# Flamingo block on one core: context 1 scaled on VectorE, x of batch 0 freed of its magic numbers on TensorE, the router's exponential moved into unit 0

## The chip, the core and the metric

One core of one Trainium2 chip. Its engines are TensorE (PE, with a weight loader, PEld), VectorE (DVE), ScalarE (ACT), GpSimd (POOL) and SyncE (SP), which issues transfers. Each runs its own list of instructions in order and waits on semaphores for the others. The metric is the time of one execution on the device, in microseconds (us).

## The reference

Four batches of 256 tokens with 256 features. The block is two gated residual steps:

```python
x = x + jnp.tanh(g_xattn[0]) * _L0_xattn_ref(_layernorm(x, axis=-1), ctx_2048)
x = x + jnp.tanh(g_ffn[0]) * _L0_ffn_ref(_layernorm(x, axis=-1), ...)
```

The first step multiplies, for each batch, the normalised x with that batch's context (256x256). Both are first rounded to 8-bit floats (4 exponent, 3 mantissa bits) and scaled back: x with one scale per token and 128 features, the context with one per 128x128 block. The second is a mixture of 8 experts of width 176 with the 4 best per token, plus a shared expert of width 704 under a sigmoid gate. The expert weights come from a softmax over router logits, so the router needs exponentials; each expert is silu(x @ wg) * (x @ wu) @ wd.

## The kernel before, in words

Everything is written out by hand: each engine has its own list, and the order in it is the order of the source.

**The attention step.** Tokens lie on the partitions, in 8 tiles of 128; a batch is two tiles. DVE takes mean and variance; ACT writes `xc`, the centred x (`centre`), and scales it to the 8-bit range (`scale_x`); contexts are scaled likewise in `cw` (`scale_ctx`, four instructions of 128 columns, one for each 128x128 block). Rounding to 3 mantissa bits is done with magic numbers: a DVE step masks the exponent bits of the value (`exponents`), a step makes of that power of two a large number (`magic` on ACT with Relu; for context 0 `magic_ctx` on DVE), and two DVE steps add it and subtract it again (`rounded`, or `round_ctx` for context 0), which leaves the rounded value in bf16 (`xq`, `cq`). For batches 0 and 1 PE transposes `xq` into PSUM (`transpose_xq`), ACT copies it to `xqt` (`copy_xqt`), and PE multiplies it with `cq` (`attend`, `attend_by_tiles`). For batches 2 and 3 transfers do the transposing.

The dequantised sum x + attention is built in parts: ACT scales the product's first half of features into `y2` (`residual0`), DVE adds the second to x (`residual1`), and a last add joins them: on POOL for batch 0 (`residual_sum_0`), on DVE for batch 1 (`residual_sum`, L812). Then come the second layer norm (`stats_x1`; `inverse_std1` on POOL, L350; `norm_x1`, L825), transposes on PE, and `h_hi` and `h_lo`, the normalised tokens as a sum of two fp32r numbers (`high_h`, `high_h_by_blocks`, `low_h`).

**Fillers.** Between the head's products PE runs products whose result nobody reads (`keep_clock_up`, L1206): 2 before `attend_by_tiles(1)`, 9 behind it, then 4, 2 and 1.

**The feed-forward step** handles the tokens in two halves of 512, and for each half the 17 slices of 128 hidden rows: 34 units, numbered n. A unit is `gate(n)` (6 products of 512 columns), `up(n)` (6) and `down(n-1)` (6), each product in three passes of high and low parts (L1143 for gate and up, L1248 to L1256 for down). ACT makes the high parts of the weights (`high_gu`, L531; `high_d`, L535), the silu and the high part of the activation (`high_a`, L552). POOL makes the low parts of the weights (`low_gu`, L362; `low_d`, L375; `low_first` for unit 0, in two pieces, L369). DVE multiplies (`gated`, L897) and makes the low part (`low_a`, L906). `gate(n)` waits for POOL's low part of its weights, and that for ACT's high part. Each half's router runs amid its first units: logits (`first_products`), `copy_logits`, transposes, `route_compare` (which ends in `ex_in`, L856, before `gt`), the exponential on ACT (`exp_router`, L515), `route_rank` (L862 to L864), `route_weigh`. Second-half batches 2 and 3 go through the attention step in between units 3 to 16 of the first half.

Silu and Exp are in different tables of ACT. A table load is an instruction of its own in the trace (ACT_TABLE_LOAD). At the start one is asked for by hand (`preload_act_table`, L438), others stand in front of the activation that needs them.

The last stage is `finish(1, ...)`: for each of two blocks of 128 output features, DVE adds the product to the residual (L936) and SP stores it.

## Time and profile before

| | |
|---|---|
| median of 3 runs | 175.09 us (174.53 to 175.18) |
| the profiled execution | 174.99 us |
| its span, first to last instruction | 172.8 us |
| mean granted TensorE clock | 1.000 |
| busy: PE, PEld | 154.2 us, 122.6 us |
| busy: DVE, ACT, POOL | 123.2 us, 103.9 us, 81.1 us |
| read from HBM, written | 21.51 MB, 1.09 MB |

An engine's busy time is the time covered by its instructions. Times of instructions count from the span's start. A row of a timeline merges neighbours of one form (x4), and in brackets gives the idle time before it and what released it. The chain of waits goes back from the last instruction to what released each step. "L1143" is line 1143 of the kernel before.

### The profile page before, as it was taken

To read this page: it belongs to the slowest core of one execution; us is meant where nothing else is said; L and a number is where in the kernel's file an instruction comes from. 1 tells how busy PE (TensorE), PEld (TensorE's weight loads), DVE (VectorE), ACT (ScalarE), POOL (GpSimd) and SP (SyncE) were. 2 spreads that over 40 slices of the span, in tenths; PEclk is the share of its full clock that TensorE was granted. 3 is DMA by queue.
4 is the path that set the end of the run, shared out by engine and by line. 5 is a ranking of instruction groups with operands and counts; after the bars stand their busy time and mean duration, and the time that the engine had idled before them with its cause. 6 is when DMAs were issued, how large, how long until landed. Compare 5 with 4: busy or idle time off the path is not lost.

```text
span 172.8 us, 2338 instructions
## 1 busy us (share of the span) xinstructions
PE 154.2 (89%) x700; PEld 122.6 (71%) x700; DVE 123.2 (71%) x258; ACT 103.9 (60%) x223; POOL 81.1 (47%) x103
## 2 busy tenths in 40 slices
PE   0033979999999999999999999999999999999991
PEld 0022447787888887877788888888888888888880
DVE  1899882897779889988989667943486655444553
ACT  2588843578668699656375545884654444554530
POOL 4350564245673565563346444353665554444410
PEclk9999999999999999999999999999999999999999
DMA  4499920000499994134423325205999100000003
GB/s 129 130 392 402 399 101 0 2 4 4 113 277 236 351 401 176 23 114 133 154 83 119 79 70 206 95 4 106 265 246 334 52 4 0 0 0 2 0 0 121
DMA packets 12768, 23.00 MB, mean 133 GB/s; under 512 B 3266, under 2 KB 4290, under 8 KB 12756
## 3 DMA queue, kind: packets, MB, share of 16 engines
q1 hardware_dynamic: 12180, 22.34, 41.1%
q10 hardware_dynamic: 576, 0.52, 1.1%
q8 instruction: 5, 0.08, 0.2%
q14 instruction: 7, 0.06, 0.1%
HBM read 21.51 MB, written 1.09 MB: 131 GB/s over the span
## 4 chain that ended last, share of the span: by engine, by line
PE 83%; DVE 6%; ACT 2%; POOL 2%; DMA 2%; issue 2%; DVEq 1%; POOLq 0%
PE bank L1143 52%; PE bank L1248 4%; PE bank L1252 4%; PE bank L1250 4%; PE bank L1249 4%; PE bank L1255 4%; PE bank L1256 4%; DMA x<-xs 2%; PE bank L1119 1%; POOL rstd L350 1%; DVE amax_x L777 1%; PE bank L1265 1%; POOL x L356 1%; ACT xc L461 1%; ACT y L486 1%
## 5 line engine op out<-in xcount | busy, mean ns | idle before, releaser
L362 POOL TENSOR_TENSOR w_lo<-w_raw,w_hi 128x512 fp32r<-128x512 f32 (+1 forms) x33 | 41.6, 1260 | 49.9 <-ACT w_hi L531 49.9
L1143 PE MATMUL bank<-h_hi,w_hi 128*128 128x512 f32 x130 | 51.5, 396 | 0.0
L1143 PE MATMUL bank<-h_hi,w_lo 128*128 128x512 f32 x130 | 50.7, 390 | 0.0
L1143 PE MATMUL bank<-h_lo,w_hi 128*128 128x512 f32 x130 | 50.6, 390 | 0.0
L552 ACT ACTIVATE a_hi<-bank 128x512 fp32r<-128x512 f32 (+1 forms) x34 | 20.3, 598 | 33.8 <-DVE bank L897 33.3
L375 POOL TENSOR_TENSOR w_lo<-w_raw,w_hi 128x256 fp32r<-128x256 f32 x33 | 24.8, 751 | 13.8 <-ACT w_hi L535 13.7
L906 DVE TENSOR_TENSOR a_lo<-bank,a_hi 128x512 fp32r<-128x512 f32 x32 | 22.0, 688 | 10.2 <-ACT a_hi L552 10.0
L897 DVE TENSOR_TENSOR bank<-silu,bank 128x512 f32<-128x512 f32 x32 | 22.2, 695 | 9.4 <-PE bank L1143 7.4
L1143 PEld LDWEIGHTS bank<-h_hi,w_hi 128*128 128x128 f32 x130 | 24.4, 188 | 5.8 <-issue 0.7
L1143 PEld LDWEIGHTS bank<-h_hi,w_lo 128*128 128x128 f32 x130 | 24.4, 188 | 5.2
L1143 PEld LDWEIGHTS bank<-h_lo,w_hi 128*128 128x128 f32 x130 | 24.4, 188 | 4.7
L884 DVE TENSOR_TENSOR silu<-bank,mix_b 128x512 f32<-128x512 f32 x22 | 15.2, 689 | 14.1 <-ACT bank L547 14.1
L531 ACT ACTIVATE w_hi<-w_raw 128x512 fp32r<-128x512 f32 (+1 forms) x34 | 20.9, 613 | 0.0
L547 ACT ACTIVATE bank<-bank 128x512 f32<-128x512 f32 x22 | 12.9, 584 | 10.7 <-PE bank L1143 10.7
L535 ACT ACTIVATE w_hi<-w_raw 128x256 fp32r<-128x256 f32 x33 | 13.6, 411 | 0.0
L1248 PE MATMUL bank<-a_hi,w_hi 128*128 128x512 f32 x30 | 11.9, 396 | 0.0
L1250 PE MATMUL bank<-a_hi,w_hi 128*128 128x512 f32 x30 | 11.7, 390 | 0.0
L1252 PE MATMUL bank<-a_lo,w_hi 128*128 128x512 f32 x30 | 11.7, 390 | 0.0
L1249 PE MATMUL bank<-a_hi,w_lo 128*128 128x512 f32 x30 | 11.7, 389 | 0.0
L1256 PE MATMUL bank<-a_lo,w_hi 128*128 128x512 f32 x30 | 11.7, 389 | 0.0
L1255 PE MATMUL bank<-a_hi,w_lo 128*128 128x512 f32 x30 | 11.7, 389 | 0.0
L543 ACT ACTIVATE silu<-bank 128x512 f32<-128x512 f32 x10 | 5.9, 594 | 4.4 <-PE bank L1143 4.4
(162 smaller groups left out, 210.9 us busy)
## 6 DMA issues: line engine op xcount, KB each, us to landing
w_raw<-w_full SPq DMA_DIRECT2D x32, 384.0 KB, 7.7
mix_b<-rows_dram SPq DMA_DIRECT2D x8, 256.0 KB, 6.5
out_t<-fin SPq DMA_DIRECT2D x4, 256.0 KB, 2.1
mix_b<-rows_dram SPq DMA_DIRECT2D x4, 224.0 KB, 6.1
mix_b<-rows_dram SPq DMA_DIRECT2D x4, 192.0 KB, 5.9
mix_b<-rows_dram SPq DMA_DIRECT2D x4, 160.0 KB, 5.8
x<-xs SPq DMA_DIRECT2D x2, 256.0 KB, 6.7
cw<-ctx_t SPq DMA_DIRECT2D x2, 256.0 KB, 7.0
```

Of the source, the lines that this page charges most:

```text
L362: nc.gpsimd.tensor_tensor(w_lo[:, n % 2, 0:cols], w_raw[:, n % RING, 0:cols], w_hi[:, n % 2, 0:cols].bitcast(F32), ALU.subtract).then_inc( ...
L375: nc.gpsimd.tensor_tensor(d_of(w_lo, d_lo_last, n), w_raw[:, n % RING, at:at + D], d_of(w_hi, d_hi_last, n).bitcast(F32), ALU.subtract).th ...
L531: nc.scalar.activation(w_hi[:, n % 2, 0:cols], w_raw[:, n % RING, 0:cols], ACT.Copy).then_inc(gu_hi_done, 1)
L552: nc.scalar.activation(a_hi[0:rows, a_slot(n), :], UP[n % 2][0:rows, :], ACT.Copy).then_inc(a_hi_done, 1)
L897: nc.vector.tensor_tensor(UP[n % 2][:], silu[:, n % 2, :], UP[n % 2][:], ALU.mult).then_inc(act_done, 1)
L906: nc.vector.tensor_tensor(a_lo[:, a_slot(n), :], UP[n % 2][:], a_hi[:, a_slot(n), :].bitcast(F32), ALU.subtract).then_inc(a_lo_done, 1)
L1143: last = nc.tensor.matmul(out, w[k][a], x_of[k][b], start=(start and k == 0 and i == 0), stop=(stop and k == blocks - 1 and i == 2))
L1248: nc.tensor.matmul(OUT[0][:], d_hi(n, 0), a_hi[:, a_slot(n), :], start=start, stop=False)
L1249: nc.tensor.matmul(OUT[0][:], d_lo(n, 0), a_hi[:, a_slot(n), :], start=False, stop=False)
L1250: nc.tensor.matmul(OUT[1][:], d_hi(n, 1), a_hi[:, a_slot(n), :], start=start, stop=False)
L1252: done = nc.tensor.matmul(OUT[0][:], d_hi(n, 0), a_lo[:, a_slot(n), :], start=False, stop=stop)
L1255: nc.tensor.matmul(OUT[1][:], d_lo(n, 1), a_hi[:, a_slot(n), :], start=False, stop=False)
```

## The change

- **Magic numbers without exponents.** The mask of the exponent bits goes. ACT takes |value| times 2^20 with Abs (`magic_x`, `magic_ctx`) into a bf16 tile (`xm`, `cm`); DVE's two rounding steps clamp it from below, add and subtract it. All contexts now go this way.
- **Context 1 scaled on DVE** (`scale_ctx1`, four instructions), not on ACT.
- **x of batch 0** is not rounded on DVE to the end: DVE clamps the magic numbers and adds them (`sum_with_magic_x`); PE transposes by products with minus identity (fp32) and identity (bf16), which add up in PSUM to the magic number less the sum, the rounded x with its sign turned (`transpose_less_sums`). The other x are rounded as magic less sum as well.
- **Orders.** ACT: `magic_x(0)` before the Tanh, `magic_ctx(0)` behind `scale_ctx(0)`, `high_gu(0)` behind `residual0(1)`. POOL: `low_first(0)` behind the residual sum. PE: one filler before `attend_by_tiles(1)` instead of two.
- **Residual sum and norm by tiles.** POOL's sum of batch 0 in two instructions, `stats_x1(0)` and the transposes of batch 1's `y2` tile by tile.
- **Router.** `exp_router(0)` stands between `silu_unit(0)` and `high_a(0)`, with loads of Exp's and Silu's tables asked for around it.
- **End.** The last unit's down goes output block by output block; the last block is finished in two halves of 256 columns, the second stored from ACT's queue.

```diff
+MAGIC = 2.0 ** 20
+LEAST = 1.5 * 2.0 ** -6
...
+            nc.gpsimd.tensor_scalar(minus_eye[:], eye[:], -1.0, None, ALU.mult).then_inc(consts, 1)
...
@@ gpsimd
-                nc.gpsimd.tensor_tensor(x1[:, tile_slice(0), :], x1[:, tile_slice(0), :], y2[:, tile_slice(0), :], ALU.add)\
-                    .then_inc(x1_ready[0], 1)
+                for j in tiles(0):
+                    nc.gpsimd.tensor_tensor(x1[:, j, :], x1[:, j, :], y2[:, j, :], ALU.add).then_inc(x1_ready[0], 1)
...
-            pool.wait_ge(cq_ready[1], 1)
-            low_first(0)
             residual_sum_0()
             low_gate_w()
+            low_first(0)
             inverse_std1(0)
...
@@ scalar
+            def magic_x(b):
+
+                a.wait_ge(x_scaled, b + 1)
+                nc.scalar.activation(xm[:, tile_slice(b)], xc[:, tile_slice(b)], ACT.Abs, scale=MAGIC).then_inc(magic_done, 1)
+
+            def magic_ctx(b):
+                a.wait_ge(ctx_scaled[b], 1)
+                nc.scalar.activation(cm[:, b], cw[:, b], ACT.Abs, scale=MAGIC).then_inc(magic_done, 1)
...
             centre(1)
+            magic_x(0)
             a.wait_ge(gates_landed, 32)
             nc.scalar.activation(g_tanh[:], g_raw[:], ACT.Tanh).then_inc(tanh_done, 1)
-            magic_x(0, 1)
             scale_ctx(0)
+            magic_ctx(0)
             scale_x(1)
-            scale_ctx(1)
-            magic_x(1, 2)
+            magic_x(1)
+            magic_ctx(1)
             copy_xqt(0)
-            magic_ctx(1, 1)
-            high_gu(0)
             copy_xqt(1)
             residual0(0)
             high_gate_w()
             residual0(1)
+            high_gu(0)
             high_d(0)
...
             copy_logits(0)
             silu_unit(0)
+            a.preload_act_table(ACT.Exp)
+            exp_router(0)
+            a.preload_act_table(ACT.Silu)
             high_a(0)
-            front(1)
-            silu_unit(1)
-            exp_router(0)
-            high_d(1)
-            high_a(1)
+            unit(1)
...
+            a.wait_ge(fin_done, KC + 3)
+            a.dma_start(out_t[1, :, HN + S:T], fin[:, 1, S:HN]).then_inc(stored, 16)
...
@@ vector
+            def rounded(views, magics, done):
+
+                val, mag, out = views
                 v.wait_ge(magic_done, magics)
...
+                after(did(nc.vector.scalar_tensor_tensor(val, mag, LEAST * MAGIC, val, ALU.max, ALU.add)))
+                nc.vector.scalar_tensor_tensor(out, mag, LEAST * MAGIC, val, ALU.max, ALU.subtract).then_inc(done, 1)
+
+            def sum_with_magic_x(b, magics):
+
+                val, mag, _ = views_x(b)
+                v.wait_ge(magic_done, magics)
+                least = nc.vector.tensor_scalar(mag, mag, LEAST * MAGIC, None, ALU.max)
+                least.then_inc(clamped, 1)
+                v.wait_ge(clamped, 1)
+                nc.vector.tensor_tensor(val, val, mag, ALU.add).then_inc(x_summed, 1)
+
+            def scale_ctx1():
+                v.wait_ge(ctx_scales, 1)
+                for i in range(2 * KC):
+                    last = nc.vector.tensor_scalar(cw[:, 1, i // 2, i % 2, :], cw[:, 1, i // 2, i % 2, :],
+                                                   scl_c[:, 0, 2 * KC + i:2 * KC + i + 1], None, ALU.mult)
+                last.then_inc(ctx_scaled[1], 1)
...
-            round_by_magic_x(0, 1)
-            mag_c0 = magic_ctx(0, exponents_ctx(0))
-            exponents_x(1)
-            round_ctx(0, mag_c0)
-            exponents_ctx(1)
-            round_by_magic_x(1, 2)
-            round_by_magic_ctx(1, 3)
+            sum_with_magic_x(0, 1)
+            scale_ctx1()
+            rounded(views_ctx(0), 2, cq_ready[0])
+            rounded(views_x(1), 3, xq_ready)
+            rounded(views_ctx(1), 4, cq_ready[1])
...
+            def finish_last(added):
+
+                after(added[0])
+                v.wait_ge(out_done, 4 * KC - 1)
+                nc.vector.scalar_tensor_tensor(fin[:, 0, :], OUT[0][:], g_tanh[:, 1:2], x1t[:, 0, HN:T], ALU.mult, ALU.add)\
+                    .then_inc(fin_done, 1)
+                after(added[1])
+                v.wait_ge(out_done, 4 * KC)
+                for half in range(2):
+                    cols = slice(half * S, (half + 1) * S)
+                    nc.vector.scalar_tensor_tensor(fin[:, 1, cols], OUT[1][:, cols], g_tanh[:, 1:2],
+                                                   x1t[:, 1, HN + half * S:HN + (half + 1) * S], ALU.mult, ALU.add)\
+                        .then_inc(fin_done, 1)
...
@@ tensor
+            def transpose_less_sums(b):
+
+                pe.wait_ge(clamped, 1)
+                pe.wait_ge(x_summed, 1)
+                for jj, j in enumerate(tiles(b)):
+                    for k in range(KC):
+                        out = QT[b][:, k * S + jj * P:k * S + (jj + 1) * P]
+                        nc.tensor.matmul(out, xc[:, j, k, :], minus_eye[:], start=True, stop=False)
+                        last = nc.tensor.matmul(out, xm[:, j, k, :], eye_b[:], start=False, stop=True)
+                last.then_inc(xqt_psum, 1)
...
             def transpose_y2_by_blocks(b):
...
+                pe.wait_ge(y2_first, 1)
+                for jj, j in enumerate(tiles(b)):
+                    if jj == 1:
+                        pe.wait_ge(y2_ready, b + 1)
+                    for k in range(KC):
+                        done = nc.tensor.transpose(Y2T1[k][:, jj * P:(jj + 1) * P], y2[:, j, k * P:(k + 1) * P], eye[:])
+                        if jj == 1:
+                            done.then_inc(y2t_psum, 1)
...
-            keep_clock_up(2)
+            keep_clock_up(1)
...
-            down(n)
+            down_block(n, 0, stop=True)
+            down_block(n, 1, stop=True)
```

In the new `down_block` the first two products wait for `a_hi`, and only the third, with the low part of the activation, for `a_lo`.

## Rows read from the trace of the kernel before

**Rows 1.** The page: busy time, share of the span and instructions of each engine
```profile
PE 154.2 (89%) x700; PEld 122.6 (71%) x700; DVE 123.2 (71%) x258; ACT 103.9 (60%) x223; POOL 81.1 (47%) x103
```

**Rows 2.** The chain of waits: by line; then start us, length us, piece
```profile
by line: PE bank L1143 51.6%; PE bank L1248 4.1%; PE bank L1252 4.1%; PE bank L1250 4.1%; PE bank L1249 4.1%; PE bank L1255 3.9%; PE bank L1256 3.9%; DMA x<-xs 1.8%; issue 1.7%; PE bank L1119 1.1%; POOL rstd L350 1.1%; DVE amax_x L777 0.8%;
...
26.16 0.47 PE bank L1179
...
39.49 2.99 PE bank L1143 x12
...
159.76 2.72 PE bank L1143 x12
```

**Rows 3.** Waits, 26 to 45 us: waiter, releaser: us, times, longest
```profile
PEld bank L1143 <- POOL w_lo L362: 0.3, 1, 0.3
```

**Rows 4.** ACT's timeline, 10 to 22 us: start, us, what [idle before]
```profile
10.67 1.28 ACT L453 ACTIVATE cw<-cw,scl_c 128x128 f32<-128x128 f32 x4
...
14.19 0.70 ACT L468 ACTIVATE xe<-xe,least 128x512 f32<-128x512 f32 x1
...
14.80 0.57 ACT L478 ACTIVATE xqt<-bank 128x512 bf16<-128x512 bf16 x1
...
17.76 1.14 ACT L486 ACTIVATE y<-bank,deq 128x128 f32<-128x128 f32 x4
...
20.37 0.69 ACT L531 ACTIVATE w_hi<-w_raw 128x512 fp32r<-128x512 f32 x1
```

**Rows 5.** DVE's timeline, 10 to 26 us
```profile
10.83 0.66 DVE L741 SCALAR_TENSOR_TENSOR xc<-xe,xc 128x512 f32<-128x512 f32 x1
...
20.34 0.75 DVE L699 BATCH_NORM_STATS2 bn<-x 128x6 f32<-128x256 f32 x2 [0.38 <-POOL x L356]
...
21.50 0.69 DVE L812 TENSOR_TENSOR x<-x,y 128x512 f32<-128x512 f32 x1
...
24.37 0.73 DVE L825 TENSOR_SCALAR y<-x,mv,rstd 128x256 f32<-128x256 f32 x2 [0.27 <-POOL rstd L350]
```

**Rows 6.** PE's timeline, 9 to 22 us (windows that part the fillers by pace)
```profile
9.40 0.59 PE L1076 MATMUL bank<-eye,blk_c 8*128 8x8 f32 x2 [0.37 <-DVE blk_c L720]
...
16.62 0.61 PE L1086 MATMUL bank<-eye_b,xq 128*128 128x128 bf16 x4 [0.16 <-DVE xq L742]
...
18.84 1.05 PE L1206 MATMUL bank<-xqt,eye_b 128*128 128x512 bf16 x2
...
19.70 1.71 PE L1206 MATMUL bank<-xqt,eye_b 128*128 128x512 bf16 x7
```

**Rows 7.** ACT's timeline, 31 to 40 us
```profile
32.00 0.60 ACT L552 ACTIVATE a_hi<-bank 128x512 fp32r<-128x512 f32 x1 [2.63 <-DVE bank L897]
...
33.63 1.28 ACT L515 ACT_TABLE_LOAD   x1
...
34.92 0.23 ACT L515 ACTIVATE ex<-ex_in 128x36 f32<-128x36 f32 x1
...
37.46 1.28 ACT L543 ACT_TABLE_LOAD   x1
```

**Rows 8.** Timelines of DVE, POOL and PE, 30 to 40 us
```profile
30.88 0.16 DVE L856 TENSOR_SCALAR ex_in<-lg 128x4 f32<-128x4 f32 x1
...
33.24 1.53 DVE L862 TENSOR_TENSOR eq<-eq,earlier 128x256 f32<-128x256 f32 x1
...
33.20 1.29 POOL L362 TENSOR_TENSOR w_lo<-w_raw,w_hi 128x512 fp32r<-128x512 f32 x1 [5.34 <-ACT w_hi L531]
...
39.19 0.27 PE L1071 MATMUL bank<-eye,amax_c 128*8 128x128 f32 x1
```

**Rows 9.** The timeline's last products and DVE steps; the page's issues of the stores
```profile
168.89 0.39 PE L1256 MATMUL bank<-a_lo,d_hi_last 128*128 128x512 f32 x1
...
168.93 1.41 DVE L936 SCALAR_TENSOR_TENSOR fin<-bank,g_tanh,x1t 128x512 f32<-128x512 f32 x2 [0.90 <-PE bank L1252]
...
out_t<-fin SPq DMA_DIRECT2D x4, 256.0 KB, 2.1
```

More of the change, by code:

```diff
@@ L462, in scale_x @@
                 last.then_inc(x_scaled, 1)
-            def magic(power, powers, count):
-                a.wait_ge(powers, count)
-                a.wait_ge(least_filled, 1)
-                nc.scalar.activation(power, power, ACT.Relu, bias=least[:], scale=MAGIC).then_inc(magic_done, 1)
-            def magic_x(b, count):
-                magic(xe[:, tile_slice(b)].rearrange("p j k c -> p (j k c)"), power_x, count)
-            def magic_ctx(b, count):
-                magic(ce[:, b].rearrange("p k n c -> p (k n c)"), power_c, count)
+            def magic_x(b):
[4 more added lines that the diff above has]
+                nc.scalar.activation(cm[:, b], cw[:, b], ACT.Abs, scale=MAGIC).then_inc(magic_done, 1)
             def copy_xqt(b):
                 a.wait_ge(xqt_psum, b + 1)
-                nc.scalar.activation(xqt[:, b], qt_view(b), ACT.Copy).then_inc(xqt_ready, 1)
+                src = QT[0][:].rearrange("p (k t) -> p k t", k=KC) if b == 0 else qt_view(b)
+                nc.scalar.activation(xqt[:, b], src, ACT.Copy).then_inc(xqt_ready, 1)
             def residual0(b):
@@ L619, in _ @@
             high_a(7)
-            magic_ctx(2, 2)
+            magic_ctx(2)
             front(8)
@@ L623, in _ @@
             scale_x(3)
-            magic_x(2, 3)
+            magic_x(2)
             high_a(8)
@@ L628, in _ @@
             scale_ctx(3)
-            magic_x(3, 4)
+            magic_x(3)
             high_a(9)
@@ L632, in _ @@
             middle(10)
-            magic_ctx(3, 3)
+            magic_ctx(3)
             high_a(10)
@@ L733, in scales_ctx @@
                 nc.vector.tensor_scalar(scl_c[:, h, :], scl_c[:, h, :], FP8_MAX, None, ALU.mult).then_inc(ctx_scales, 1)
-            def exponents(mag, val):
-                return nc.vector.tensor_scalar(mag.bitcast(I32), val.bitcast(I32), EXP_BITS, None, ALU.bitwise_and)
-            def rounded(out, val, power, magics, done):
-                v.wait_ge(magic_done, magics)
-                after(did(nc.vector.scalar_tensor_tensor(val, power, LEAST, val, ALU.add, ALU.add)))
-                nc.vector.scalar_tensor_tensor(out, val, LEAST, power, ALU.subtract, ALU.subtract).then_inc(done, 1)
@@ L754, in exponents_ctx @@
-            def exponents_ctx(b):
-                v.wait_ge(ctx_scaled, b + 1)
-                last = exponents(ce[:, b].rearrange("p k n c -> p (k n c)"), cw[:, b].rearrange("p k n c -> p (k n c)"))
-                if b > 0:
-                    last.then_inc(power_c, 1)
-                    return None
-                return did(last)
-            def magic_ctx(b, exponents_step):
-                after(exponents_step)
-                mag = ce[:, b].rearrange("p k n c -> p (k n c)")
-                return did(nc.vector.tensor_scalar(mag, mag, SUBNORMAL, MAGIC, ALU.max, ALU.mult))
@@ L815, in stats_x1 @@
             def stats_x1(b):
-                v.wait_ge(x1_ready[b], 1)
-                moments(1, x1, b, mean1_ready)
+                if b == 0:
+                    for jj, j in enumerate(tiles(0)):
+                        v.wait_ge(x1_ready[0], jj + 1)
+                        step = did(nc.vector.bn_stats(bn[:, 1, j, :], x1[:, j, :]))
+                else:
+                    v.wait_ge(x1_ready[b], 1)
+                    step = None
+                moments(1, x1, b, mean1_ready, step)
                 v.wait_ge(mean1_ready, b + 1)
@@ L826, in norm_x1 @@
                                                    ALU.subtract, ALU.mult)
+                    if b == 1 and j < BT * b + 1:
+                        last.then_inc(y2_first, 1)
                 last.then_inc(y2_ready, 1)
@@ L1132, in transpose_y2_by_blocks @@
             def transpose_y2_by_blocks(b):
-                pe.wait_ge(y2_ready, b + 1)
-                for k in range(KC):
-                    for jj, j in enumerate(tiles(b)):
-                        last = nc.tensor.transpose(Y2T1[k][:, jj * P:(jj + 1) * P], y2[:, j, k * P:(k + 1) * P], eye[:])
-                    last.then_inc(y2t_psum, 1)
+                pe.wait_ge(y2_first, 1)
[6 more added lines that the diff above has]
+                            done.then_inc(y2t_psum, 1)
             def three_passes(out, w, x_of, start, stop):
@@ L1258, in down, with down_block @@
                     done.then_inc(out_done, 1)
-            def down_block(n, k):
+            def down_block(n, k, stop=False):
                 pe.wait_ge(d_lo_done, n + 1)
+                pe.wait_ge(a_hi_done, n + 1)
+                nc.tensor.matmul(OUT[k][:], d_hi(n, k), a_hi[:, a_slot(n), :], start=False, stop=False)
+                nc.tensor.matmul(OUT[k][:], d_lo(n, k), a_hi[:, a_slot(n), :], start=False, stop=False)
                 pe.wait_ge(a_lo_done, n + 1)
-                for w, act in ((d_hi(n, k), a_hi), (d_lo(n, k), a_hi), (d_hi(n, k), a_lo)):
-                    nc.tensor.matmul(OUT[k][:], w, act[:, a_slot(n), :], start=False, stop=False)
+                done = nc.tensor.matmul(OUT[k][:], d_hi(n, k), a_lo[:, a_slot(n), :], start=False, stop=stop)
+                if stop:
+                    done.then_inc(out_done, 1)
             def unit(n):
```

94 lines of the change are left out of this document (36 added, 58 removed).

## The prediction

> **What bounds the kernel now.** The page's busy line comes first: the tensor engine (PE) has 89% of the span, no other engine over 71% [rows 1]. So a microsecond counts only where PE is idle or does work that is not its own. The chain of waits says where [rows 2]: PE's line 1143 is 51.6% of it, almost all that belongs to other engines lies before 26.16, where the first feed-forward product starts, and from there PE issues products of 512 columns 0.227 us apart (12 in 2.72). Three places are left: the head (0 to 26.16), the few holes in PE's stream behind it, and the tail after the last product at 168.89. The view of waits from 26 to 45 us names one hole, 0.3 us in which PE's weight load waited for POOL's w_lo, which ended at 34.49: unit 2's gate [rows 3, 8]. PE's timeline has another: L1071 starts at 39.19, the next gate only at 39.49; a silu behind a table load (37.46 + 1.28, then some 0.6) ends at 39.35 [rows 2, 7, 8]. Last come the timelines of the head, engine by engine [rows 4, 5, 6], and the tail [rows 9].
>
> **The head.** Removed from DVE: the exponent step of x 0, ctx 0, x 1, ctx 1, and ctx 0's magic step. Added on DVE: a clamp on bf16 and four scalings of 128 columns. On ACT four scalings leave, magic_ctx(0) comes, and every magic step stands right behind its scaling.
>
> ACT now sets the pace. scale_ctx(0) still waits for the scales, starts at 10.67 and ends at 11.95. A magic step costs what L468 does, 0.61 start to start (14.19 to 14.80); Abs is taken at Relu's price, four scalings at L453's 1.28 [rows 4]. So magic_ctx(0) starts at 11.99, scale_x(1) runs 12.60 to 13.87, magic_x(1) starts at 13.90, magic_ctx(1) at 14.51, copy_xqt(0) runs 15.12 to 15.70; it ran 14.80 to 15.37, so it is 0.32 later.
>
> DVE has room. The clamp starts where L741 did, at 10.83. It has no row: more than nothing, at most L741's 0.66 for the same columns; I take half. With a sum of 0.69 x 0 is summed at 11.9 (12.2). The four scalings: L825 takes 0.73 for two of 256 columns, so four of 128 lie between 0.73 (the same columns) and 1.46 (the same step four times); I take 0.8, near the first, since L478 beside L468 shows that the steps overlap [rows 4, 5]. At either, a rounding (two steps of 0.69) of ctx 0, x 1 and ctx 1 is paced by ACT's magic steps: ready at 14.1 (at the most 14.6), 16.05 and 17.4.
>
> PE's fp32 products with minus_eye have no row of their size. Below them stand the four transposes they replace (0.61); nearest is L1076's pair, two issues for one fp32 product in 0.59, about 0.23 apart; above, eight issues at the slow 512-column step, 0.43, and four bf16 of a quarter of it, together 3.9 [rows 6]. I take the nearest: 4 x (2 x 0.23 + 0.11) = 2.3, done at 14.2, covered by ACT until 15.12. At 3.9 it would end at 15.8 and cost 0.7.
>
> attend(0) then starts at 15.75 instead of 15.42, four products of 256 columns 0.21 apart, so x 1's transposes come at 16.6; they started at 16.62, held by xq [rows 6]. ACT's y of batch 0 stays at 17.76 to 18.90 [rows 4]: what DVE won, ACT's order has taken. POOL's residual sum waits for that y, so it starts at 19.02 again. Cut in two tiles (0.73 for one, 0.69 apart, from half of L812's columns at POOL's pace in L362, 1.29 for 512) it ends at 20.43, not 20.31. But bn_stats has tile 0 done by then and ends at 20.88 instead of 21.09 [rows 5]: 0.21 won. Half goes again. high_gu(0) now stands behind ACT's y of batch 1, where the next step starts at 20.05, takes 0.69 [rows 4] and ends at 20.74; POOL's low_first(0), moved ahead of inverse_std1(0), runs 20.80 to 21.53 and reads SBUF, while DVE wants to start L812, with both operands in SBUF, at 21.28. The rows show what then happens: L862 (256 columns, both operands in SBUF) started 0.04 after POOL's L362, took 1.53 and ended 0.28 after it [rows 8]. So L812 ends at 21.53 + 2 x 0.28 = 22.08, where it ended at 22.19: 0.11 won. The variance and the norm of batch 1 follow: 24.26 for 24.37. y2_first lets tile 0's transposes run under tile 1's norm, so the block that high_h needs lacks one transpose instead of two, 0.11 more. First product: 26.16 - 0.11 - 0.11 = 25.94. **Head: -0.22.**
>
> **The router's exponential.** Before, it stood behind silu(1), with loads of 1.28 at 33.63 and 37.46. Now Exp's load follows silu(0) and falls into the 2.63 that ACT was idle before a_hi [rows 7]. Silu's load doesn't. Counted without the head's gain: ex_in is ready at 31.04, the exponential runs 31.08 to 31.31 (0.23), Silu's load to 32.61, high_a(0) starts at 32.62 and not at 32.00: +0.62 [rows 7, 8]. Behind it on ACT stands high_gu(2), behind that POOL's w_lo, then gate(2), which already waited for w_lo [rows 3]; so gate(2) starts 0.62 later. DVE's low_a(0), L862, act(1) and the maxima of contexts 2 and 3 queue behind a_hi and move with it; down(0)'s waits for a_hi and a_lo fall inside the same 0.62. In unit 2 the load of 37.46 is gone: PE is free for gate(3) 0.05 after L1071's start at 39.19 and finds silu done, not at 39.49: -0.25. **Router: +0.62 - 0.25 = +0.37.**
>
> One rule is weighed here. The rows show 1.28 for each load [rows 7]. The Trainium skill (ScalarE: Activation LUTs, section Table sets: the hidden batching unit) gives about 2.7 for one; by that a_hi would come some 2.0 later, not 0.62. The trace disagrees with it, and the sum goes by the trace.
>
> **The tail.** In the new order the third of the last six products needs a_lo, before it was the fourth: between nothing and one product (0.227); I take 0.09. The third starts at 168.89 - 3 x 0.227 = 168.21 and DVE does the first block under the rest. The second block's halves start after PE's end (169.28 + 0.09), at 169.44; half of 0.70 apart they end at 170.23, where L936 ended at 170.34. The last store holds 128 KB; 256 KB took 2.1 to land, and how much of that is size no row tells: between nothing and half, of which PE's and DVE's order leaves at most 0.3; I take 0.06 [rows 9]. **Tail: -0.17**, from 0 to -0.45.
>
> **Edits at no cost.** The exponents of contexts and x 2 and 3 lie beside a PE that waits for none of them. minus_eye is one small step in POOL's start-up, and its consumers come after 8 us. The store on ACT's queue and down_block's split waits have nothing behind them.
>
> Sum: 174.99 (the profiled execution) - 0.22 + 0.37 - 0.17 = 174.97; the runs' median, 175.09, is 0.10 above. I forecast **175.0**. A measurement of this kernel tells about 0.5% (0.9 us) from no change.
>
> **Rivals.**
> (a) The head wins more. PE ran at 1.2 GHz until 19.70 (0.43 start to start) and at 2.4 GHz behind it (seven in 1.71) [rows 6]; the granted clock stands at 1.000 all along. With 2.3 us of products where 0.61 stood, it may be at 2.4 GHz for attend(0): half of 0.85 saved, and y and the residual sum come 0.43 earlier, 174.5. Against it: a microsecond and a half of idleness is still ahead of attend(0). 12%.
> (b) The clock comes later. With one filler less PE is idle from 17.44 to 17.93, ahead of attend(1). If the rise moves behind the nine fillers, each costs 0.21 more, PE is late for y2's transposes by 0.9 and high_h by 0.7: 175.7. 12%.
> (c) Silu's load is hidden after all: -0.22 - 0.25 - 0.17, 174.35. Against it: between ex_in (31.04) and a_hi (32.00) there is 0.96, and exponential and load need 1.55. 6%.
> (d) The other side: Abs is not in the table set of Silu and Tanh. No row has Abs; Relu, Identity, Copy and Tanh ran without a load. If it is not, loads stand before magic_x(0), the Tanh and magic_ctx(0), some +3 in the head, and two in each of four units, 2.6 on an ACT that is 60% busy [rows 1], so 1.6 free in a unit's 18 x 0.227 = 4.1: +4. About 182; it decides from the first load in the head on. 3%.
> (e) A load takes twice the row: the exponential held to 31.7 and 1.28 more behind it, 177.2. The Trainium skill's figure, same page and section, comes to this; both loads in the trace speak against it. 1%.
> The main case has 63%, its own range 174.5 to 175.4; 3% are for what I don't see. To leave out no more than 2 in 10 the range takes in (a), (b) and the 0.7 of slow fp32 products: 174.2 to 175.8. Faster by over 0.5% needs (a) with (c), or head and tail at their best ends: 12%. Slower: (d), (e), or (b) with the slow products: 9%. The rest, 79%, is no difference.
>
> **What would show it.** The first xqt copy at about 15.1; L812 stretched by low_first(0); the first product near 25.9; one load right behind the exponential, a hole of 0.5 to 0.7 in PE before gate(2), near 34.9; none before gate(3). Wrong if a load stands before an Abs, if 0.43 steps go on past 20, or if gate(2) starts without waiting.

## The result, and the profile after

The kernel after runs in 175.13 us (median of 22 executions, 175.01 to 175.40 and one at 176.93), the kernel before, beside it, in 174.87 (median of 22). The ratio is 1.002 (95% interval 1.0011 to 1.0028). That is 0.35 us slower (the medians differ by 0.26), inside the forecast range (174.2 to 175.8) and inside the 0.5% that was called no difference, but on the other side of zero from the -0.02 that the sum gave. That the total lies as near to the forecast as it does is partly luck: two gains, 0.25 and 0.17, never came, and 0.17 that the sum didn't have (0.10 more in the head, 0.07 in the long stretch behind it) stands against them. Two executions of the kernel before, beside the experiments, took 273.85 and 411.99 us; they are in no ratio and in no count below.

The profiled execution took 175.07 us, span 173.3, granted clock 0.999. Set against the one of before (174.99 us), stretch by stretch:

| stretch, us | before | after | forecast change | measured change |
|---|---|---|---|---|
| x lands (the first bn_stats starts) | 3.83 | 4.02 | 0 | +0.19 |
| to the first product | 22.33 | 22.01 | -0.22 | -0.32 |
| to gate(2) | 8.38 | 9.02 | +0.62 | +0.64 |
| to gate(3) | 4.95 | 4.95 | -0.25 | 0 |
| to the start of the last product | 129.40 | 129.33 | 0 | -0.07 |
| to the end of the execution | 6.10 | 5.74 | -0.17 | -0.36 |
| of it outside the span | 2.19 | 1.77 | 0 | -0.42 |

When x lands varies from execution to execution, whatever the kernel (3.82 to 4.53 over the 14 profiles of this study), so the head is read from there. The stretches from there to the last product repeat within 0.07 us wherever their code is the same, which makes them a finer ruler than the time of an execution. The last rows need care. The tail that the forecast speaks of is the part inside the span, 3.91 and 3.97 us, the same within the 0.1 to which spans are given. What differs lies outside the span, between the time of the execution and that from its first to its last instruction, and E7 shows that it varies among the executions of one and the same kernel. From x's landing to the last product the change is -0.32 + 0.64 + 0 - 0.07 = +0.25, and with a tail that changes nothing this is what the medians show.

**The head.** The page's busy line:

```profile
PE 156.1 (90%) x707; PEld 124.3 (72%) x707; DVE 119.6 (69%) x252; ACT 102.4 (59%) x220; POOL 81.2 (47%) x104
```

PE's share went from 89% to 90% [rows 1], DVE and ACT gave up 3.6 and 1.5 us of work, and neither fact says anything about the time. ACT's timeline from 9 to 21 us (start, us, what):

```profile
9.41 0.61 ACT L466 ACTIVATE xm<-xc 128x512 bf16<-128x512 f32 x1
...
10.93 1.27 ACT L452 ACTIVATE cw<-cw,scl_c 128x128 f32<-128x128 f32 x4 [0.81 <-DVE scl_c L730]
12.24 0.63 ACT L470 ACTIVATE cm<-cw 128x512 bf16<-128x512 f32 x1
...
14.07 0.63 ACT L466 ACTIVATE xm<-xc 128x512 bf16<-128x512 f32 x1
14.60 0.61 ACT L470 ACTIVATE cm<-cw 128x512 bf16<-128x512 f32 x1
15.12 0.58 ACT L475 ACTIVATE xqt<-bank 128x512 bf16<-128x512 f32 x1
```

No load stands before an Abs (L466, L470). The first copy of xqt starts at 15.12 as forecast, though the scales came 0.26 later than before (10.93 for 10.67), 0.19 of it with x: a magic step goes on to the next after 0.53 (14.07 to 14.60), not the 0.61 of [rows 4], and there are three of them on the way. PE has time, by little:

```profile
12.23 0.77 PE L1095 MATMUL bank<-minus_eye,xc 128*128 128x128 f32 x2 [1.98 <-DVE xc L756]
...
14.71 0.31 PE L1096 MATMUL bank<-eye_b,xm 128*128 128x128 bf16 x1
15.76 1.03 PE L1112 MATMUL bank<-cq,xqt 128*128 128x256 bf16 x4 [0.73 <-ACT xqt L475]
...
26.03 0.47 PE L1193 MATMUL bank<-h_hi,gate_hl 128*128 128x512 f32 x1 [0.24 <-ACT h_hi L500]
```

The four groups stand 0.64 apart and end at 15.02, 0.10 before ACT comes to the copy (2.8 us; forecast 2.3, at most 3.9). attend(0) follows at 15.76, at the pace of before. Then DVE and POOL meet over the residual sum (DVE's timeline, then POOL's, 20 to 25 us):

```profile
21.21 0.36 DVE L809 TENSOR_SCALAR ve<-mv 128x2 f32<-128x2 f32 x1
21.49 0.68 DVE L796 TENSOR_TENSOR x<-x,y 128x512 f32<-128x512 f32 x1
...
24.35 0.73 DVE L815 TENSOR_SCALAR y<-x,mv,rstd 128x256 f32<-128x256 f32 x2 [0.27 <-POOL rstd L350]
```

```profile
19.02 1.41 POOL L357 TENSOR_TENSOR x<-x,y 128x256 f32<-128x256 f32 x2 [6.28 <-ACT y L483]
...
20.82 0.73 POOL L369 TENSOR_TENSOR w_lo<-w_raw,w_hi 128x256 fp32r<-128x256 f32 x1 [0.19 <-ACT w_hi L528]
```

low_first(0) does get in the way (20.82 to 21.55), but what it holds is the small step ahead of the sum, L809, 0.36 instead of 0.17. The sum (L796) starts behind it at 21.49 and runs undisturbed to 22.17; forecast 22.08. Counted from x's landing it ends 18.15 after it, where the forecast has 18.25 (22.08 - 3.83) and the kernel before 18.36.

**The router.** ACT's timeline from 29 us on, and the row of the view of waits, 26 to 45 us:

```profile
29.27 1.28 ACT L590 ACT_TABLE_LOAD   x1
30.96 0.23 ACT L512 ACTIVATE ex<-ex_in 128x36 f32<-128x36 f32 x1 [0.41 <-DVE ex_in L848]
31.21 1.28 ACT L592 ACT_TABLE_LOAD   x1
32.51 0.60 ACT L549 ACTIVATE a_hi<-bank 128x512 fp32r<-128x512 f32 x1
...
37.24 0.60 ACT L549 ACTIVATE a_hi<-bank 128x512 fp32r<-128x512 f32 x1 [2.83 <-DVE bank L889]
```

```profile
PEld bank L1157 <- POOL w_lo L362: 0.6, 1, 0.6
```

This is the forecast step, 0.64 for 0.62: a_hi at 32.51 where it was 32.00, with a first product 0.13 earlier; the wait for w_lo 0.6 where it was 0.3 [rows 3]. The load costs its 1.28 and the next activation starts 0.02 behind its end. The Trainium skill (ScalarE: Activation LUTs, section What ACT_TABLE_LOAD costs) gives 1.28 for the load itself as well, and 1.38 more for draining the engine around it; no such gap is in this trace.

The -0.25 isn't there. DVE, POOL and PE, 33 to 40 us:

```profile
33.75 1.53 DVE L854 TENSOR_TENSOR eq<-eq,earlier 128x256 f32<-128x256 f32 x1
35.31 0.85 DVE L855 TENSOR_TENSOR gt<-gt,eq 128x256 f32<-128x256 f32 x1
...
36.53 0.69 DVE L889 TENSOR_TENSOR bank<-silu,bank 128x512 f32<-128x512 f32 x1
```

```profile
33.70 1.29 POOL L362 TENSOR_TENSOR w_lo<-w_raw,w_hi 128x512 fp32r<-128x512 f32 x1 [5.87 <-ACT w_hi L528]
34.95 0.93 POOL L375 TENSOR_TENSOR w_lo<-w_raw,w_hi 128x256 fp32r<-128x256 f32 x1
```

```profile
35.05 0.50 PE L1157 MATMUL bank<-h_hi,w_hi 128*128 128x512 f32 x1 [0.17 <-POOL w_lo L362]
...
37.68 0.39 PE L1157 MATMUL bank<-h_hi,w_lo 128*128 128x512 f32 x1
37.99 0.47 PE L1262 MATMUL bank<-a_hi,w_hi 128*128 128x512 f32 x1
...
38.75 0.46 PE L1266 MATMUL bank<-a_lo,w_hi 128*128 128x512 f32 x1
39.05 0.40 PE L1269 MATMUL bank<-a_hi,w_lo 128*128 128x512 f32 x1
...
39.95 0.27 PE L1070 MATMUL bank<-eye,amax_c 128*8 128x128 f32 x1
40.00 0.47 PE L1157 MATMUL bank<-h_hi,w_hi 128*128 128x512 f32 x1
```

gate(3) does start 0.05 behind L1070: the hole of [rows 8] is closed. But PE now loses as much before it. From the last product of up(2) (37.68) to the router's transposes behind down(1) (39.51) it takes 1.83, before 1.59 (37.17 to 38.76), in three steps of 0.30 or 0.31 where the pace is 0.23: at the start of down(1), behind its first product, and at its a_lo. The view of waits has a row there that the kernel before doesn't have:

```profile
PEld bank L1266 <- DVE a_lo L898: 0.2, 1, 0.2
```

Upstream stand a_hi(1) at 37.24 and act(1) (L889) at 36.53, and ahead of that the step L855, 0.85 long. The same step and the same POOL step in the kernel before:

```profile
34.80 0.42 DVE L863 TENSOR_TENSOR gt<-gt,eq 128x256 f32<-128x256 f32 x1
```

```profile
35.54 0.74 POOL L375 TENSOR_TENSOR w_lo<-w_raw,w_hi 128x256 fp32r<-128x256 f32 x1 [1.05 <-ACT w_hi L535]
```

While L855 runs, POOL now runs low_d(1) (L375, 34.95 to 35.88), directly behind w_lo. high_d(1), which feeds it, stood behind the exponential and a load before; the move has made it early.

**The tail.** The timeline's last steps, and the page's view of transfers from 169 us on (KB each, us from issue to landing):

```profile
169.33 0.40 PE L1281 MATMUL bank<-a_lo,d_hi_last 128*128 128x512 f32 x1
169.83 0.88 DVE L934 SCALAR_TENSOR_TENSOR fin<-bank,g_tanh,x1t 128x256 f32<-128x256 f32 x2
```

```profile
out_t<-fin SPq DMA_DIRECT2D x1, 128.0 KB, 2.2
out_t<-fin ACTq DMA_DIRECT2D x1, 128.0 KB, 2.1
```

The two halves end at 170.71, 1.38 behind the last product's start; forecast 1.25 (170.23 for 168.98), before 1.45. And 128 KB land no sooner than 256 KB [rows 9]. The 0.07 is not to be found at the end of the span.

### The profile page after: what moved, and what is told of

Read it like the earlier page. It is cut to its first block, busy times and chain, and to the rows that moved or that the text cites. A ratio compares the mean times of both kernels' runs of the same rounds, so it can differ in the third digit from the quotient of the medians.

```text
span 173.3 us, 2339 instructions
## 1 busy us (share of the span) xinstructions
PE 156.1 (90%) x707; PEld 124.3 (72%) x707; DVE 119.6 (69%) x252; ACT 102.4 (59%) x220; POOL 81.2 (47%) x104
## 4 chain that ended last, share of the span: by engine, by line
PE 82%; DVE 6%; ACT 5%; DMA 2%; issue 2%; POOL 2%; DVEq 0%; POOLq 0%
PE bank L1157 49%; PE bank L1262 4%; PE bank L1266 4%; PE bank L1264 4%; PE bank L1269 4%; PE bank L1263 4%; PE bank L1270 4%; DMA x<-xs 2%; PE bank L1129 2%; PE bank L1112 1%; POOL x L357 1%; POOL w_lo L362 1%; ACT cw L452 1%; ACT xc L460 1%; ACT cm L470 1%
## 5 line engine op out<-in xcount | busy, mean ns | idle before, releaser
L375 POOL TENSOR_TENSOR w_lo<-w_raw,w_hi 128x256 fp32r<-128x256 f32 x33 | 24.6, 745 | 12.8 <-ACT w_hi L532 12.7
L889 DVE TENSOR_TENSOR bank<-silu,bank 128x512 f32<-128x512 f32 x32 | 22.2, 695 | 9.1 <-PE bank L1157 7.0
L1070 PE MATMUL bank<-eye,amax_c 128*8 128x128 f32 x2 | 0.6, 323 | 8.8 <-DVE amax_c L690 8.8
```

The source lines that it names most:

```text
L375: nc.gpsimd.tensor_tensor(d_of(w_lo, d_lo_last, n), w_raw[:, n % RING, at:at + D], d_of(w_hi, d_hi_last, n).bitcast(F32), ALU.subtract).th ...
L889: nc.vector.tensor_tensor(UP[n % 2][:], silu[:, n % 2, :], UP[n % 2][:], ALU.mult).then_inc(act_done, 1)
```

## The experiments

Each was timed in five rounds against the kernel before. "After" in a heading means that the edit is made to the kernel after. The table has what the traces show, in the stretches of the table above; the last column is the part of the one before it that lies outside the span.

| kernel | ratio (95%) | to first product | to gate(2) | to gate(3) | to last product | to the end | outside the span |
|---|---|---|---|---|---|---|---|
| before | 1 | 22.33 | 8.38 | 4.95 | 129.40 | 6.10 | 2.19 |
| after | 1.0020 (1.0011 to 1.0028) | 22.01 | 9.02 | 4.95 | 129.33 | 5.74 | 1.77 |
| E1 router back | 0.9997 (0.9979 to 1.0015) | 22.01 | 8.39 | 4.95 | 129.30 | 5.74 | 1.81 |
| E2 router alone | 1.0045 (1.0029 to 1.0061) | 22.32 | 9.00 | 4.95 | 129.42 | 6.08 | 2.15 |
| E3 tail back | 1.0022 (1.0013 to 1.0030) | 22.02 | 9.01 | 4.96 | 129.31 | 5.74 | 1.85 |
| E4 w_hi before a_hi | 1.0013 (0.9985 to 1.0041) | 22.02 | 8.51 | 4.64 | 129.36 | 6.83 | 1.81 |
| E5 low_first behind | 1.0030 (1.0008 to 1.0052) | 21.88 | 9.02 | 4.95 | 129.33 | 5.72 | 1.81 |
| E6 high_d behind a_hi | 1.0054 (1.0035 to 1.0072) | 22.02 | 9.01 | 5.50 | 129.35 | 5.73 | 1.81 |
| E7 head alone | 0.9969 (0.9956 to 0.9981) | 22.03 | 8.39 | 4.95 | 129.31 | 5.73 | 1.80 |
| E8 best | 0.9961 (0.9944 to 0.9978) | 21.86 | 8.51 | 4.63 | 129.36 | 5.73 | 1.77 |
| E9 E4, old end | 0.9962 (0.9949 to 0.9975) | 22.02 | 8.51 | 4.63 | 129.32 | 5.88 | 1.92 |
| E10 E4, halves on SP | 0.9983 (0.9961 to 1.0006) | 22.01 | 8.51 | 4.67 | 129.37 | 5.72 | 1.74 |
| E11 E5, old end | 1.0007 (0.9994 to 1.0020) | 21.85 | 9.01 | 4.95 | 129.34 | 5.73 | 1.80 |
| E12 E4's order on before | 0.9981 (0.9967 to 0.9996) | 22.33 | 8.50 | 4.67 | 129.40 | 6.06 | 2.09 |

**E1: after, the router's order as before.**

```diff
             silu_unit(0)
-            a.preload_act_table(ACT.Exp)
-            exp_router(0)
-            a.preload_act_table(ACT.Silu)
             high_a(0)
-            unit(1)
+            front(1)
+            silu_unit(1)
+            exp_router(0)
+            high_d(1)
+            high_a(1)
```

> The changed kernel with the router's exponential back behind silu(1) and no loads asked for by hand. Theory 1 (the router's part is what costs: in the traces gate(3) starts 0.52 later than before although the first product starts 0.13 earlier): the head's gain is left alone, 174.5 us, ratio to before 0.998, gate(2) without a hole of its own. Rival (the loss is the tail's, the span's last 0.4 us, and the router's part is neutral): about 175.1, as the changed kernel.

Measured: 174.82 us (174.39 to 175.00, and two at 176.11 and 176.12, which are in its interval). To gate(2) 8.39 again, the wait for w_lo 0.3 again, so the 0.64 is the order's. What the head wins by itself the wide interval doesn't tell; E7 does.

**E2: before, the new router order alone.**

```diff
             silu_unit(0)
-            high_a(0)
-            front(1)
-            silu_unit(1)
+            a.preload_act_table(ACT.Exp)
             exp_router(0)
-            high_d(1)
-            high_a(1)
+            a.preload_act_table(ACT.Silu)
+            high_a(0)
+            unit(1)
```

> The kernel before with the router's new order alone. Theory 1: gate(2) 0.5 to 0.6 later, nothing won back before gate(3), 175.4 to 175.5 us, ratio 1.0035. Rival (my forecast: the hole before gate(3) closes and gives 0.25 back): +0.37, 175.2. Rival of the neutral router: 174.9.

Measured: 175.69 us, 0.67 above the median of before beside it (175.02). By its trace +0.62 to gate(2) and nothing back to gate(3). The view of waits has

```profile
PEld bank L1142 <- POOL w_lo L362: 0.6, 1, 0.6
```

and L855's counterpart takes 0.84 (POOL's low_d(1) again directly behind w_lo). So the order costs 0.6 by itself; the change's other parts have no share in the lost -0.25.

**E3: after, the end as before** (down not block by block, the last block finished and stored whole).

```diff
-            down_block(n, 0, stop=True)
-            down_block(n, 1, stop=True)
+            down(n)
...
-            finish_last(shared_1)
+            finish(1, shared_1)
...
-            a.wait_ge(fin_done, KC + 3)
-            a.dma_start(out_t[1, :, HN + S:T], fin[:, 1, S:HN]).then_inc(stored, 16)
```

> The changed kernel with the old end (the old order of the last six products, one store per block, all from the same queue). Theory 1 (the tail gains nothing and costs nothing: two half steps of 0.48 take as long as one of 0.75, a store of 128 KB lands in 2.1 as one of 256 KB): 175.1, as the changed kernel, within 0.1. My forecast's tail gain (0.17): 175.3. Rival (the tail loses 0.4): 174.7.

Measured: 175.44 us, ratio 1.0022, that of after; 5.74 from the last product to the end with either end, 3.9 to 4.0 of it inside the span. The tail's term is 0, and the 0.36 that the kernel after is shorter there isn't its tail.

**E7: after with E1's and E3's edits, so the head alone.**

```diff
-            a.preload_act_table(ACT.Exp)
-            exp_router(0)
-            a.preload_act_table(ACT.Silu)
             high_a(0)
-            unit(1)
+            front(1)
+            silu_unit(1)
+            exp_router(0)
+            high_d(1)
+            high_a(1)
...
-            finish_last(shared_1)
+            finish(1, shared_1)
...
-            down_block(n, 0, stop=True)
-            down_block(n, 1, stop=True)
+            down(n)
```

> The changed kernel with the router's order and the end as before, so the head's changes alone. Theory (head gains 0.2 to 0.3, the new end nothing): 0.2 to 0.3 less than the kernel before, ratio 0.9985. Rival (the head gains nothing, what the run with the router put back won came from the end): ratio 1.000.

Measured: 174.63 us (174.31 to 175.05), 0.5 us faster than before; the interval reaches from 0.33 to 0.77. The stretches from x's landing to the last product add up to -0.38 (-0.30, +0.01, 0, -0.09), inside it. The column to the end has 5.73 against 6.10, but from the last product's start to the end of the span both take 3.9 (172.7 - 168.77, 172.8 - 168.89), so the 0.37 lies outside the span.

It isn't the head's. The page's view of queues counts the fetches of instructions inside the span. For queue 8 it has the first of these rows in before, E2, E12 and E9, and the second in the ten other kernels:

```profile
q8 instruction: 5, 0.08, 0.2%
```

```profile
q8 instruction: 6, 0.10, 0.2%
```

In the four the sixth fetch, 16 KB, stands behind the end of the span (in before between 174.2 and 174.4). They have 1.92 to 2.19 us outside the span, the ten others 1.74 to 1.85, and E9 has the new head. One kernel has executions of either kind: 2.0 us or more stand outside the span in 26 of 99 executions of before, in three of E12's twelve (old head) and in five of E11's twelve (new head). It is more frequent with the old head (33 of 118 executions of before, E2 and E12, against 13 of 130 of all others), but a difference between two single profiles says nothing of the head. That the late fetch is what lengthens an execution is likely by these four profiles and not shown; what sets its time stays open.

**E6: after, high_d(1) behind high_a(1)**, to take low_d(1) out of DVE's way.

```diff
-            unit(1)
+            front(1)
+            silu_unit(1)
+            high_a(1)
+            high_d(1)
```

> The changed kernel with high_d(1) behind high_a(1) on ACT, so that POOL's low_d(1) doesn't stand right behind its w_lo of unit 2. Theory (my forecast of 0.25 back before gate(3) failed because low_d(1), early now, holds up DVE's gt + eq, 0.85 instead of 0.42, and so act(1), a_hi(1) and PE's down(1)): gt + eq takes 0.42, a_hi(1) comes 0.4 earlier, PE's three small waits in down(1) go, 0.2 less than the changed kernel. Rival (act(1) is late because of the loads alone): gt + eq stays at 0.85 or down(1) waits as before, no difference.

Measured: 176.02 us, worse. DVE's row, POOL's, and the wait:

```profile
35.39 0.42 DVE L858 TENSOR_TENSOR gt<-gt,eq 128x256 f32<-128x256 f32 x1
```

```profile
37.89 0.73 POOL L375 TENSOR_TENSOR w_lo<-w_raw,w_hi 128x256 fp32r<-128x256 f32 x1 [2.81 <-ACT w_hi L532]
```

```profile
PEld bank L1265 <- POOL w_lo L375: 0.9, 1, 0.9
```

The collision is gone, L858 takes 0.42 and a_hi(1) starts at 36.91, 0.33 earlier than in the kernel after (0.41 counted from x's landing). That is what shows that low_d(1) stretched the step and with it held a_hi(1). But high_d(1) now waits for a_hi(1), and down(1) needs its low part: PE waits 0.9 for it. The first cure put the same work on the path from the other side. That PE's small waits in down(1) go once the step is short is therefore not shown here: another wait covers them.

**E4: after, w_hi of unit 2 between the exponential and a_hi, Silu's load behind a_hi.**

```diff
             exp_router(0)
-            a.preload_act_table(ACT.Silu)
+            front(1)
             high_a(0)
-            unit(1)
+            a.preload_act_table(ACT.Silu)
+            middle(1)
+            high_a(1)
```

> The changed kernel with high_gu(2) ahead of high_a(0), and Silu's load behind high_a(0), since neither is a Silu. Theory 1 (gate(2) waits for w_lo of unit 2, which stands behind Silu's load): w_lo ends near 33.2 instead of 35.0, silu(1) ends near 34.3, no hole before gate(2) or gate(3): 0.6 to 0.9 less than the changed kernel, 174.2 to 174.5, ratio 0.997. Rival (it is the load itself, wherever it stands): 175.1.

Measured: two groups, six executions at 174.26 to 174.63 and six at 175.71 to 176.71. The stretches say what the order does: to gate(2) 8.51, to gate(3) 4.64, 0.82 less than after together and 0.18 less than before. high_a and high_gu need no table of their own (both ran with Exp's loaded), so the load is no longer ahead of them; POOL's w_lo ends at 33.42, before DVE reaches the pair at 33.47, and its two steps take 0.42 and 0.43. The upper group is taken up under E9.

**E12: before, with E4's order.**

```diff
             silu_unit(0)
-            high_a(0)
-            front(1)
-            silu_unit(1)
+            a.preload_act_table(ACT.Exp)
             exp_router(0)
-            high_d(1)
+            front(1)
+            high_a(0)
+            a.preload_act_table(ACT.Silu)
+            middle(1)
             high_a(1)
```

> The kernel before with the exponential in unit 0, high_gu(2) ahead of high_a(0) and Silu's load behind it; head and end as before. Theory (the place of Silu's load in ACT's order is what costs; behind both steps that are no Silu, it costs less than the two loads of before): from the first product to gate(3) 13.15 us, where the kernel before has 13.33 and the changed kernel 13.97, so 0.2 less than before, ratio 0.999. Rival (the exponential in unit 0 costs wherever the load stands): the 0.4 to 0.6 more that the router's part alone showed (1.0045).

Measured: 174.90 us, ratio 0.9981 against E2's 1.0045. The same exponential in the same unit costs 0.6 or gives a little, by the order of ACT's steps around it. Two things differ from E2: Silu's load stands behind w_hi and a_hi, and w_hi stands ahead of a_hi. No run has one of them alone. The load isn't hidden altogether either: silu(1) now stands behind it and ends at 35.22, long after POOL's w_lo (33.90), and gate(2) starts at 35.36, 8.50 behind the first product, in the kernel before 8.38.

**E5: after, low_first(0) behind inverse_std1(0), as it stood before the change; E11: the same with the old end.**

```diff
             residual_sum_0()
             low_gate_w()
-            low_first(0)
             inverse_std1(0)
+            low_first(0)
```

> The changed kernel with POOL's low_first(0) behind inverse_std1(0) instead of ahead of it. Theory (low_first(0) on POOL, 20.8 to 21.5 us, holds up DVE's step for the variance, 0.36 instead of 0.17, and with it the residual sum of batch 1, and so takes back half of what the tiles of batch 0 won): that step takes 0.17 again, first product 0.15 to 0.2 earlier, 0.2 less than the changed kernel. Rival (the two don't meet in a shared resource, the order is free): no difference in that step's duration or in time.

> The changed kernel with low_first(0) behind inverse_std1(0) and the old end: with the new end its trace showed the step of 0.17 and the first product 0.13 earlier by its own start, while its times scattered from 174.8 to 176.6. Theory: with the old end the scatter goes, and it stands 0.1 to 0.3 below the changed kernel with the old end (ratio 1.0022), so about 1.001. Rival (the scatter belongs to POOL's order): it stays.

Measured: E5 175.59 us, scattered from 174.81 to 176.62; E11 175.20 (174.70 to 175.98). The traces have the gain:

```profile
21.12 0.17 DVE L809 TENSOR_SCALAR ve<-mv 128x2 f32<-128x2 f32 x1
21.20 0.69 DVE L796 TENSOR_TENSOR x<-x,y 128x512 f32<-128x512 f32 x1
```

L809 is back at 0.17, and the first product comes 21.88 and 21.85 after x, not 22.01. The time of E5 doesn't have it; with the end of before it is there (1.0007 against E3's 1.0022), though the intervals overlap.

**E9: E4 with the old end; E10: E4 with the second half's store on SP's queue.** E4's upper group came with the new end, so one takes the new end away and one only ACT's queue.

```diff
-            a.wait_ge(fin_done, KC + 3)
-            a.dma_start(out_t[1, :, HN + S:T], fin[:, 1, S:HN]).then_inc(stored, 16)
...
+            sp.wait_ge(fin_done, KC + 3)
+            sp.dma_start(out_t[1, :, HN + S:T], fin[:, 1, S:HN]).then_inc(stored, 16)
```

> The version with high_gu(2) ahead of high_a(0), with the old end (two stores of 256 KB, both on SP's queue). It had two groups of times with the new end, 174.3 to 174.6 and 175.7 to 176.7; its profile was of the second and showed a 16 KB instruction fetch at 170.25 for 1.3 us amid the stores, and the last store, on ACT's queue, landed after 3.2 us instead of 2.1. Theory A (the new end makes the kernel open to it: the last store is small, late and on a queue of its own): one group alone, 174.3 to 174.6 median, ratio 0.996. Theory B (the fetch comes at that time whatever the end is): two groups again, about 1 us apart.

> The version with high_gu(2) ahead of high_a(0), the new end in halves, but the second half's store on SP's queue too. Theory A1 (it is ACT's queue): one group, 174.3 to 174.6. Theory A2 (it is the halves, or B, the fetch): two groups again. If the profile is of the long group it shows a fetch in the stores, and the landing of the store that it met.

Measured: E9 174.44 us, all within 174.22 to 174.64. E10 174.57, ten within 174.26 to 174.80 and two at 175.77 and 176.32. So the upper group goes with the halves, not with ACT's queue. E4's profile was taken in the upper group; its view of transfers from 169 us on (packets, MB and share by queue, then issues):

```profile
q8 instruction: 1, 0.02, 1.4%
...
out_t<-fin SPq DMA_DIRECT2D x1, 256.0 KB, 2.4
out_t<-fin SPq DMA_DIRECT2D x1, 128.0 KB, 2.3
out_t<-fin ACTq DMA_DIRECT2D x1, 128.0 KB, 3.2
```

A fetch of 16 KB of instructions ran from 170.24 to 171.56, amid the stores, and the last store landed after 3.2 us, not 2.1; the span ends 5.0 us behind the last product's start, not 3.9 to 4.0. In the profile of E9 the last fetch falls behind the stores, in E10's, one of the lower group, ahead of them (near 165). Of the other kernels with the new end, E1 has two of twelve executions 1.1 us above its others, and after one of 22, 1.5 above; no kernel with the old end has such a gap between its spans. This is one profile of an execution of that group: that every one of the upper group has this cause, and why the fetch falls there more often in E4 and E5 than in after, stays open.

**E8: the best of the parts**: the new head with low_first(0) behind inverse_std1(0), E4's order, the old end.

```diff
-            low_first(0)
             inverse_std1(0)
+            low_first(0)
...
-            a.preload_act_table(ACT.Silu)
+            front(1)
             high_a(0)
-            unit(1)
+            a.preload_act_table(ACT.Silu)
+            middle(1)
+            high_a(1)
...
-            finish_last(shared_1)
+            finish(1, shared_1)
...
-            down_block(n, 0, stop=True)
-            down_block(n, 1, stop=True)
+            down(n)
```

> The version that the findings point to: the changed kernel's head with low_first(0) behind inverse_std1(0), high_gu(2) ahead of high_a(0) with Silu's load behind it, and the old end. Theory (head -0.3 to -0.5, the holes before gate(2) and gate(3) closed, -0.3): 174.2 to 174.4, ratio 0.996. If some executions are 1.5 us longer, as half of those of the version with high_gu(2) ahead were, and that comes from an instruction fetch of 16 KB that falls into the last stores, the profile shows its time; with stores of 256 KB on one queue it would cost the same. Rival (that came with the store on ACT's queue): no execution is longer by 1.5 us.

Measured: 174.34 us (174.07 to 175.14), ratio 0.9961, 0.7 us below before. ACT's timeline:

```profile
31.17 0.23 ACT L511 ACTIVATE ex<-ex_in 128x36 f32<-128x36 f32 x1 [0.41 <-DVE ex_in L847]
31.31 0.62 ACT L527 ACTIVATE w_hi<-w_raw 128x512 fp32r<-128x512 f32 x1
32.10 0.60 ACT L548 ACTIVATE a_hi<-bank 128x512 fp32r<-128x512 f32 x1 [0.17 <-DVE bank L888]
32.72 1.28 ACT L593 ACT_TABLE_LOAD   x1
34.01 0.60 ACT L539 ACTIVATE silu<-bank 128x512 f32<-128x512 f32 x1
```

w_hi fills the time that ACT waited for DVE, a_hi waits 0.17 for its input instead of for a load, and the load stands in the time until silu(1), which it delays: silu(1) ends at 34.61, and gate(2) starts at 34.75. E9 (0.9962) can't be told from it.

## Why the prediction missed, step by step

- **The head, -0.22: too small.** Measured from x's landing it is -0.32, and so in the seven other kernels whose head is the same (22.01 to 22.03). The mis-sized term is the magic step, 0.53 apart and not 0.61, three times, worth 0.24: the copy of xqt comes 11.10 after x's landing, forecast 11.29 (the scales took back 0.07 of it, 6.91 for 6.84). Of this 0.19, 0.10 is left at the residual sum, for low_first(0) on POOL cost more than forecast. The mechanism was right there (POOL's step holds DVE), but the victim was L809, and it lost 0.17 of what the tiles of batch 0 had won (bn_stats ends 0.38 earlier than before, counted from x, the sum 0.21), forecast 0.10. The 0.11 of y2_first fits: norm of batch 1 0.02 earlier than before, the first product 0.13. In this one execution x came 0.19 late and hid most of it.
- **The router, +0.62: right,** in place, cause and size (+0.64; +0.62 in E2), with every rival for it, (c), (d) and (e), refuted by the same rows.
- **The router, -0.25: the step that failed.** "In unit 2 the load of 37.46 is gone" held, and gate(3) starts 0.05 behind L1070 as stated. But "move with it" was taken as a plain shift of everything behind a_hi. Not all moved alike: high_d(1) lost the load ahead of it, so low_d(1) moved up against w_lo and stretched L855 to 0.85, which held act(1) and a_hi(1), and down(1) paid what gate(3) won. In the terms of the sum it is a cost that was put at nothing: what high_d(1) would do at its new place. It measured 0.43 on L855 and 0.24 on PE, all of the gain. E6 shows the stretch and that a_hi(1) hangs on it; E2 that the loss belongs to the order alone; E4 and E12, where the pair runs free and the load stands elsewhere, that the 0.3 before gate(3) can be had. That the stretch by itself is the 0.24 is read from the rows of down(1) and was not measured alone.
- **The tail, -0.17: the second step that failed.** The price of half a step and the share of size in a store's landing were taken too well: halves are 0.40 apart and not 0.35, the step of 256 columns takes 0.48, and 128 KB land in 2.1 as 256 KB do, where 0.06 was forecast. a_lo cost PE 0.02, not 0.09. E3 measures the whole term as 0.
- **Rivals (a) and (b), the clock.** The granted clock is 0.999 and attend(0) keeps its slow pace (four in 1.03). The fillers' row:

```profile
18.73 2.42 PE L1220 MATMUL bank<-xqt,eye_b 128*128 128x512 bf16 x9
```

Seven at the fast step took 1.71 before [rows 6], so nine in 2.42 leave 0.71 for the first two, and PE is at 2.4 GHz from about 19.5 on (before 19.70). Neither rival came.
- **What no term had:** -0.07 between gate(3) and the last product. The kernels with the new head have 129.30 to 129.37 there, those with the old one 129.40 to 129.42; in which of its steps it lies no run tells. The -0.36 behind the last product is no part of the change (E7).

## What to carry to other kernels

- An activation that needs no table of its own (here the copies that make w_hi and a_hi) is better put ahead of a table load than behind it, and the load directly before the step that needs it. Here that, together with w_hi ahead of a_hi, is the difference between 1.0045 and 0.9981; the share of each was not measured.
- When a step leaves a queue, ask not only what is behind its new place but what moves up at its old one, and on which engine that lands: two POOL steps back to back can hold a DVE step that a gap between them let through.
- A gain of tenths is read best from stretches between instructions in the trace, which repeated within 0.07 us here while x's landing alone varied by 0.7 and the time outside the span by 0.8 (1.74 to 2.58). Before a difference at either end of two profiles is put down to the code, look at how the executions of one kernel spread there.

## What was not expected of the hardware

- A DVE step of 128x2 with one operand in SBUF is held by a POOL step as well (L809, 0.36 for 0.17), not only the wide ones with two.
- Two DVE steps behind two POOL steps back to back take 1.53 and 0.85 where they take 0.41 and 0.42 alone, and POOL's second takes 0.93 for 0.73. The Trainium skill (SBUF — State Buffer, section SBUF: two separate sides) calls the port that both use an exclusive lock, held by whichever starts first for its whole instruction; the rows agree for DVE, whose two steps end 0.29 and 0.28 behind the ends of POOL's.
- Halving a store from 256 to 128 KB saved nothing of its 2.1 us, and a 16 KB fetch of instructions among the last stores went with a landing of 3.2.
- The time outside the span isn't a constant: 1.74 to 1.98 us in most executions and 2.0 to 2.6 in others of the same kernel (E11: seven and five of twelve).
